# Cross attention: keys turned by DVE in blocks and placed by transfers through DRAM, for every batch but the first

## The reference

```python
q = x @ Wq.T
k_raw = context @ Wk.T          # context: 16 x 361 x 512
v_raw = context @ Wv.T
# heads of 16, 32 of them; k and v are the even and odd columns of [k_raw, v_raw]
q = _rmsnorm(q); k = _rmsnorm(k)      # t * rsqrt(mean(t*t over the 16) + 1e-6)
scores = einsum('bhnd,bhmd->bhnm', q, k) * 16 ** -0.5
out = einsum('bhnm,bhmd->bhnd', softmax(scores), v)
x = x + out
```

## Time and profile before

| | |
|---|---|
| median of 3 runs | 1312.95 us (1312.74 to 1315.94) |
| the profiled execution's own time | 1312.68 us |
| its span, first to last instruction | 1310.9 us |
| instructions | 27154 |
| busy: PE, DVE, ACT, POOL | 97%, 60%, 50%, 23% of the span |
| transfers | 63.98 MB in 18744 packets, mean 49 GB/s |

### The profile page before, as it was taken

One profiled execution on the slowest core, in us unless ns is written; L12 is line 12 of the kernel. 1 busy time (PEld: TensorE's weight loads), 2 busy tenths in 40 slices (PEclk: granted clock), 3 DMA queues, 4 the chain that ended last, 5 costly groups with the idle time before them and its releaser, 6 DMA issues.

```text
span 1310.9 us, 27154 instructions
## 1 busy us (share of the span) xinstructions
PE 1268.3 (97%) x10784; PEld 850.2 (65%) x10784; DVE 781.7 (60%) x1890; ACT 648.9 (50%) x1524; POOL 295.8 (23%) x293
## 2 busy tenths in 40 slices
PE   8989999999999999999999999999999999999998
PEld 7656666666666666566666666666666665666554
DVE  6897788777877787434344434554455784443423
ACT  4663344343433356377777776666665523232221
POOL 0564454334334451111101101111101121000000
PEclk9999999999999999999999999999999999999999
DMA  8102000000000021112222222001012310000000
GB/s 330 73 9 73 9 8 10 7 3 9 9 8 9 9 88 63 72 32 84 105 73 73 74 73 89 25 25 58 25 58 84 125 52 24 1 24 1 24 1 30
DMA packets 18744, 63.98 MB, mean 49 GB/s; under 512 B 1850, under 2 KB 3386, under 8 KB 15418
## 3 DMA queue, kind: packets, MB, share of 16 engines
q1 hardware_dynamic: 18618, 62.24, 13.4%
HBM read 55.68 MB, written 3.28 MB: 45 GB/s over the span
## 4 chain that ended last, share of the span: by engine, by line
PE 83%; DVE 6%; issue 5%; ACT 4%; POOL 2%; DMA 0%; POOLq 0%; SPq 0%; DVEq 0%; ACTq 0%
PE A L1861 18%; PE A L1761 11%; PE C L2214 10%; PE A L1824 10%; PE C L1892 6%; PE B L1912 4%; PE C L1789 3%; PE A L2233 3%; PE A L1842 3%; PE B L2233 2%; PE C L1806 2%; PE A L1770 2%; PE B L1781 2%; PE B L1878 1%; PE B L1797 1%
## 5 line engine op out<-in xcount | busy, mean ns | idle before, releaser
L1861 PE MATMUL A<-wxhl,arena 128*126 128x512 f16 x1104 | 254.7, 381 | 3.2 <-DVE arena L1221 2.6
L1861 PEld LDWEIGHTS A<-wxhl,arena 128*126 128x126 f16 x1104 | 145.4, 136 | 86.3 <-issue 8.1
L1761 PE MATMUL A<-arena,wxhl 128*125 128x512 f16 (+1 forms) x780 | 174.5, 380 | 1.3 <-DVE tub L1140 1.3
L855 ACT ACTIVATE arena<-C 126x1600 f32<-126x1600 f32 x96 | 144.4, 1504 | 22.3 <-PE C L1892 22.3
L595 POOL TENSOR_TENSOR arena<-arena,region 126x512 f32<-126x512 f32 (+2 forms) x59 | 60.9, 1062 | 405.8 <-DVE region L1282 405.8
L1761 PEld LDWEIGHTS A<-arena,wxhl 128*125 128x125 f16 (+1 forms) x780 | 103.5, 136 | 62.1 <-DVE tub L1140 5.3
L2214 PE MATMUL C<-arena 128*128 128x375 f16 (+1 forms) x768 | 138.8, 333 | 0.0
L758 ACT ACTIVATE region<-C,negm 100x100 f32<-100x100 f32 x256 | 84.3, 358 | 100.8 <-DVE negm L1183 100.8
L569 POOL TENSOR_TENSOR region<-tub 125x512 f32<-125x512 f32 (+1 forms) x65 | 82.5, 1269 | 219.3 <-DVE tub L1140 217.0
L1824 PE MATMUL A<-arena,stageb 128*125 128x512 f16 (+1 forms) x416 | 124.0, 379 | 2.1 <-ACT qk L829 1.3
L2214 PEld LDWEIGHTS C<-arena 128*128 128x128 bf16 x768 | 74.8, 97 | 58.8
(11 more groups left out here) (201 smaller groups left out, 2256.5 us busy)
## 6 DMA issues: line engine op xcount, KB each, us to landing
stageb<-in_wffn SPq DMA_DIRECT2D x16, 768.0 KB, 4.8
arena<-in_ctxt SPq DMA_DIRECT2D x16, 756.0 KB, 5.8
stageb<-in_wffn SPq DMA_DIRECT2D x8, 1024.0 KB, 6.2
arena<-in_wqkv SPq DMA_DIRECT2D x4, 1024.0 KB, 12.1
wxhl<-in_wffn SPq DMA_DIRECT2D x4, 1024.0 KB, 4.7
arena<-in_wx SPq DMA_DIRECT2D x3, 1024.0 KB, 8.4
out_x<-xres SPq DMA_DIRECT2D x12, 224.0 KB
xres<-in_wo SPq DMA_DIRECT2D x2, 1024.0 KB, 19.3
```

What stands on the lines that cost most here:

```text
L855: act.activation(e[:, at:at + 2].rearrange("p f (r s) -> p r f s", r=RT), Call[0:KC, :].rearrange("p (r x) -> p r x", r=RT)[:, :, 0:4 * S] ...
L1761: ins = pe.matmul(A[j % 2][0:m, :], xp[:, k, at:at + m], wp[:, j, k, :], start=(n == 0), stop=(n == 11))
L1861: ins = pe.matmul(A[(par + n) % 2][0:KC, :], xp[:, k, c * KC:(c + 1) * KC], wp[:, 1 if n < 4 else 2, k, :], start=(i == 0), stop=(i == 11))
```

## The change

For every batch but the first, keys are no longer turned by PE. DVE transposes the normed key tile raw[par][:, c] (128 x 512) in blocks of 32 x 32 into a staging tile kts[:, c] (turn_keys). SP then writes the staging tile to a DRAM buffer with four transfers, one for each block of 32 partitions (keys_out), whose addresses put each block of 32 x 32 at its place in the turned matrix: runs of 32 words of 4 bytes. The buffer for c = 0 and 1 is kd01, for c = 2 kd2, each twice, by the parity of the batch. When the writes have landed, one transfer reads kd01 into kTd, the new tile of turned keys, and another the batch's own columns of kd2 (keys_in); a third reads the shared tile's tail into the next batch's half of kTd (keys_shared). PE's scores wait for these transfers (kr01 ahead of unit 0; kr2 and krx ahead of unit 1). Batch 0 still goes through PE and ACT.

The norms are worked out in two parts of 64 columns (key tiles 0 and 1; key tile 2 and queries), each with its own signal to POOL, which now takes key tiles 0 and 1, then queries, then key tile 2. On DVE the ternary passes stand behind the second part, and turn_keys of tile 2 behind add_cross of the first half. PE's wait for last turn's add_cross moves from ahead of turn_heads(b,2) to ahead of x2_turn.

The diff, cut to its core:

```diff
-        kT = carve([128, 2, NT, CTXP])
+        kTd = carve([128, 2, NT, NC * KP])
...
+        kd01 = nc.dram_tensor("keys01", (2, 128, NT, 2, KP), F32).ap()
+        kd2 = nc.dram_tensor("keys2", (2, 128, NT, KP), F32).ap()
...
+            def keys_out(b, c):
+
+                sp.wait_ge(*count("d_kt", b, c + 1))
+                for n in range(4):
+                    block = slice(32 * n, 32 * n + 32)
+                    if c < 2:
+                        dst = kd01[b % 2].rearrange("(r j) t c n -> c j t r n", r=4)[c][:, :, :, block]
+                    else:
+                        dst = kd2[b % 2].rearrange("(r j) t n -> j t r n", r=4)[:, :, :, block]
+                    sp.dma_start(dst, kts[block, c].rearrange("j (t r i) -> j t r i", t=NT, r=4)).then_inc(kw[c], 16)
+
+            def keys_in(b):
+
+                for c in range(2 if short(b) else NC):
+                    keys_out(b, c)
+                sp.wait_ge(*written(0, b))
+                sp.wait_ge(*written(1, b))
+                sp.wait_ge(*count("pe_sc", b - 2, NU))
+                sp.dma_start(kTd[:, b % 2, :, 0:2 * KP], kd01[b % 2].rearrange("p t c n -> p t (c n)")).then_inc(kr01, 16)
+                if not short(b):
+                    sp.wait_ge(*written(2, b))
+                    own = own_rows(b)
+                    sp.dma_start(kTd[:, b % 2, :, 2 * KP:2 * KP + own], kd2[b % 2][:, :, 0:own]).then_inc(kr2, 16)
+
+            def keys_shared(b):
+
+                sp.wait_ge(*count("pe_sc", b - 1, NU))
+                own = own_rows(b)
+                src = kd01[b % 2][:, :, 1] if short(b) else kd2[b % 2]
+                sp.dma_start(kTd[:, 1 - b % 2, :, 2 * KP + own:2 * KP + KC], src[:, :, own:KC]).then_inc(krx, 16)
...
             for b in range(NB - 2):
                 if b < NB // 2:
                     sixteenth(2 * b, 0)
+                if b > 0:
+                    keys_shared(b)
+                if b < NB // 2:
                     sixteenth(2 * b + 1, 1)
                 context(b + 2)
+                keys_in(b + 1)
                 if b == NB // 2:
...
+            keys_shared(NB - 2)
...
                 tile(n)
+                if n == 3:
+                    keys_in(NB - 1)
...
-                pool.wait_ge(*count("d_rstd2", b, 1))
                 q = [(rows_of(q_tile(b)), 3, "g_qn")] if q_tile(b) is not None else []
                 last = 1 if short(b) else 2
-                for rows, slot, done in q + [(KC, c, "g_kn") for c in range(last + 1)]:
+                keys = [(KC, c, "g_kn") for c in range(last + 1)]
+                for rows, slot, done in keys[:2] + q + keys[2:]:
+                    pool.wait_ge(*count("d_rstd2", b, 1 if slot < 2 else 2))
...
-                    act.wait_ge(*count("pe_T", b - 2, 4))
+                    if b == 2:
+                        act.wait_ge(pe_T0, NT)
+                    act.wait_ge(*count("d_kt", b - 2, 3))
...
-            def keys_back(b, t):
-
-                act.wait_ge(*count("pe_T", b, t + 1))
-                own = own_rows(b)
-                tail = (1 if short(b) else 2) * KC
-                whole = 2 * KC if short(b) else tail + own
-                ins = act.activation(kT[:, b % 2, t, 0:whole], B[0][:, 0:whole], ACT.Copy)
-                if b < NB - 1:
-                    act.wait_ge(*count("pe_sc", b - 1, T_UNITS[t]))
-                    ins = act.activation(kT[:, 1 - b % 2, t, 2 * KC + own:CTXP], B[0][:, tail + own:tail + KC], ACT.Copy)
-                ins.then_inc(sig["a_T"], 1)
+            def first_keys_back(t):
+
+                act.wait_ge(pe_T0, t + 1)
+                own = own_rows(0)
+                act.activation(kTd[:, 0, t].rearrange("p (c n) -> p c n", c=NC)[:, :, 0:KC],
+                               B[0][:, 0:CTXP].rearrange("p (c n) -> p c n", c=NC), ACT.Copy)
+                act.activation(kTd[:, 1, t, 2 * KP + own:2 * KP + KC], B[0][:, 2 * KC + own:CTXP], ACT.Copy)\
+                   .then_inc(a_T0, 1)
...
-            def rms_start(b, par):
-
-                if q_tile(b) is not None:
+            def rms_start(b, part, par):
+
+                if part == 1 and q_tile(b) is not None:
                     dve.wait_ge(*count("d_ssqq", q_tile(b), 1))
-                dve.wait_ge(*count("d_ssq2", b, 3))
+                dve.wait_ge(*count("d_ssq2", b, 2 + part))
                 dve.wait_ge(*count("g_kn", b - 2, 3))
-                st.chain(dve.tensor_scalar(xssq, xssq, 1.0 / XD,
-                                           EPS_RMS * (SX * SW) ** 2, ALU.mult, ALU.add))
-                y = xrstd[par].bitcast(I32)
-                st.chain(dve.tensor_scalar(y, xssq.bitcast(I32), 1, None, ALU.logical_shift_right))
+                v = xssq[:, 64 * part:64 * part + 64]
+                st.chain(dve.tensor_scalar(v, v, 1.0 / XD, EPS_RMS * (SX * SW) ** 2, ALU.mult, ALU.add))
+                y = xrstd[par][:, 64 * part:64 * part + 64].bitcast(I32)
...
+            def turn_keys(b, c, par):
+
+                dve.wait_ge(*count("g_kn", b, c + 1))
+                dve.wait_ge(*written(c, b - 1))
+                dve.transpose(kts[:, c], raw[par][:, c])\
+                   .then_inc(sig["d_kt"], 2 if c == 1 and short(b) else 1)
...
+                if end < 2:
+                    rms_start(b + 1, 0, odd)
+                    for n in range(3):
+                        rms_step(0, odd, n == 2)
+                    if not short(b + 1):
+                        square_sums(b + 1, 3)
+                    turn_keys(b + 1, 0, odd)
+                    turn_keys(b + 1, 1, odd)
+                    rms_start(b + 1, 1, odd)
+                    for n in range(3):
+                        rms_step(1, odd, n == 2)
                 if b == NB // 2 + 1:
                     scales3()
                 if NB // 2 < b < NB - 1:
                     ternary(*divmod(b - NB // 2 - 1, 2))
-
-                if end < 2:
-                    if not short(b + 1):
-                        square_sums(b + 1, 3)
-                    rms_start(b + 1, odd)
-                    for n in range(3):
-                        rms_step(odd, n == 2)
-                else:
+                if end == 2:
...
                     add_cross(o2_tile(b), 0)
+                if end < 2 and not short(b + 1):
+                    turn_keys(b + 1, 2, odd)
...
-                    pe.wait_ge(*count("a_T", b, 1))
                     pe.wait_ge(*count("d_qT", last_tile(b), 1))
+                if b == 0 and u != 2 and u < 5:
+                    pe.wait_ge(a_T0, {0: 1, 1: 2, 3: 3, 4: 4}[u])
+                elif b > 0 and u == 0:
+                    pe.wait_ge(kr01, 16 * b)
+                elif b > 0 and u == 1:
+                    pe.wait_ge(*own_landed(b))
+                    if b == 1:
+                        pe.wait_ge(a_T0, 4)
+                    else:
+                        pe.wait_ge(krx, 16 * (b - 1))
...
-                if last_o2(b - 1) >= 0:
-                    pe.wait_ge(*count("d_on", last_o2(b - 1), 2))
-                elif b == 0:
+                if b == 0:
                     pe.wait_ge(*count("d_x2", 1, 1))
-                turn_heads(b, 2, par)
+                    turn_heads(0, 2, 0)
...
-                pe.wait_ge(*count("a_T", b, 3))
-                turn_heads(b, 3, par)
+                if b == 0:
+                    pe.wait_ge(a_T0, 3)
+                    turn_heads(0, 3, 0)
...
-                    if q_tile(b + 1) is not None:
-                        pe.wait_ge(*count("d_qT", q_tile(b + 1), 1))
-                    turn_heads(b + 1, 0, odd)
...
-                if end < 2:
-                    turn_heads(b + 1, 1, odd)
...
-                if end < 2:
-                    pe.wait_ge(*count("a_T", b + 1, 2))
+                if end < 2 and q_tile(b + 1) is not None:
+                    pe.wait_ge(*count("d_qT", q_tile(b + 1), 1))
```

More of the change, by code:

```diff
@@ L260, in build @@
         carve = carver()
-        raw = [carve([KC, 4, 512]) for _ in range(2)]
+        raw = [carve([128, 4, 512]) for _ in range(2)]
         ctxs = carve([128, KT, CTXP])
@@ L435, in build, with written, own_landed @@
         g_ones = sem("g_ones")
+        pe_T0, a_T0 = sem("pe_T0"), sem("a_T0")
+        kw = [sem(f"kw{c}") for c in range(NC)]
+        kr01, kr2, krx = sem("kr01"), sem("kr2"), sem("krx")
+        def written(c, b):
+            return kw[c], 4 * 16 * sum(c < 2 or not short(n) for n in range(1, b + 1))
+        def own_landed(b):
+            return kr2, 16 * sum(not short(n) for n in range(1, b + 1))
         d_warm, a_ws, g_wlo, a_z = sem("d_warm"), sem("a_ws"), sem("g_wlo"), sem("a_z")
@@ L1580, in _ @@
                 square_sums(0, n)
-            rms_start(0, 0)
-            for n in range(3):
-                rms_step(0, n == 2)
+            for part in range(2):
+                rms_start(0, part, 0)
+                for n in range(3):
+                    rms_step(part, 0, n == 2)
             normed2(1, rs1[:, 0:1])
@@ L1891, in scores2 @@
```

(16 more changed lines are left out.)

42 lines of the change are left out of this document (23 added, 19 removed).

## The result

The changed kernel takes **1386.24 us**, the median of 5 runs (1382.83 to 1387.51), against 1312.95 before; the ratio of the means, here as for every run below, is 1.0544, with a 95% interval of 1.0526 to 1.0563. It is 73 us slower; the prediction said 1409, with 1338 to 1540 as its range. Its profiled execution took 1387.05 us, with a span of 1385.3.

What follows compares the result with a forecast made beforehand. PE (TensorE), busy 97% of the span, was taken as the bound. 1312.7 - 24.3 (work off PE) + 80 (waits for keys) + 7 (ternary) + 33 (clock) = 1409 us, range 1338 to 1540.

Steps and rivals of the forecast that it cites:

- What goes from PE: Cross attention on PE: 172 transposes of keys and the 0.21 us waits for ScalarE's copy go, 24.3 us less.
- Wait for keys: PE's first scores of a batch wait for the keys' read: 5.0 us in 13 turns, 7.7 in two, 80 us.
- cheap packets: Rival for the keys' writes: at 7 to 15 ns a packet SP's order alone sets the wait; 1352 us, chance 0.25.
- x2_lo: Ternary passes on DVE now stand ahead of x2_lo, so PE's out_turn comes later in turns 9 to 14: 7 us.
- just covered: Turn 1: x2_lo ends at 604.6, when PE's out_turn wants it; each tenth of a slower step is paid.
- Clock: PE runs at a lower clock after each wait for keys: 2.2 us times 15, 33 us.
- 20 to 40 ns, 0.48: The forecast's own case for the price of a 128-byte packet, summed at 30 ns to 1409 us; chance 0.48.
- The signs: Expected in the profile: 15 waits for keys of 5 us, none for the second read, some 88,000 packets under 512 bytes.
- Hidden transfers: Rival: group 2's turn to the read's landing takes at most 3.2 us, PE never waits; 1296 us, chance 0.04.
- break-even: Case where group 2's turn to the read's landing takes about 4.8 us and the change gains nothing; chance 0.04.
- costs nothing but order: Extra DVE work of 2.4 us of norms and 2 us of turns a turn, in an engine busy 14 of 32 us.
- Dear packets: Rival for the keys' writes: about 50 ns a packet, waits of 12.6 us a turn, 189 us; 1510 us, chance 0.19.

Runs made afterwards that it cites:

- e3: The changed kernel without the three reads of turned keys and PE's waits for them, so scores work on zeros: 1318.64 us, ratio 1.0047.
- e2: The changed kernel with the read of groups 0 and 1 issued ahead of the four writes of group 2: 1333.63 us, ratio 1.0169.
- e5: The changed kernel with group 2 written by eight transfers of 16 partitions instead of four of 32, same 128-byte runs: 1417.9 us, ratio 1.0782.
- e4: The changed kernel with the ternary passes moved from between the norms and x2_lo to behind queries_back: 1380.66 us, ratio 1.0513.
- e1: The changed kernel with 14 products of unused result on PE ahead of its wait for the keys, batches 1 to 14: 1372.75 us, ratio 1.0454.
- e6: The changed kernel with the read ahead of group 2's writes, ternary passes behind queries_back, x2_lo ahead of the norms' second part: 1327.66 us, ratio 1.0109.
- e8: e6 with the read of groups 0 and 1 cut in two, 128 KB for unit 0 first, then the rest: 1315.5 us, ratio 1.0012.
- e9: e8 with ten products of unused result ahead of the first scores of the two short batches: 1311.78 us, ratio 0.9985.

## Why the prediction came out as it did

The direction, the first late step and the order of its causes were right. Of the four terms of the sum one was far off, one was half of what it should have been, and they erred in opposite directions. That the total came within 23 us is in part luck.

**What goes from PE: 24.3 predicted, 25.1 measured.** 172 transposes at 0.116 us (e3; 0.125 was taken) are 19.9 us, the 13 waits for ACT's copy 2.8. Not counted in the prediction were two waits of turn_heads for the turned queries, the 1.4 and 1.0 in the earlier trace rows, which also went: 2.4. The busy times agree: 21.0 us less at full rate.

**Wait for keys: 80 predicted, 47.9 measured.** The chain was the one described: second sum, norms (12 steps from 599.44 to 602.44, 3.0 us, 3.1 predicted), POOL (2.08 for two products), turns (0.71 each against 0.65), add_cross, the turn of group 2, four issues, the read, the scores. Two sizes in it were off. The mis-sized term is **the packet**: 30 ns was taken, 11.7 measured, so nothing queued behind the packets and the range's far end, 108 ns, was never near. What looked like a fixed cost of 23 ns in the difference between 2 KB writes and reads the earlier trace rows wasn't one. The other is the issue: 0.65 us against 0.59 taken. The wait of turn 1 is thus that of the rival "cheap packets", 3.0 worked out there and 3.36 measured; SP's order makes it, as e2 and e5 show from either side. Nor were the turns ahead of short batches the dear ones: 7.7 was predicted, measured were 4.0 in turn 6 and none in turn 13. There PE waits 4.9 us for x2_lo earlier in the turn, which covers it; the prediction priced each wait as though the other weren't there.

The page "DMA: Bandwidth & Descriptors" of the Trainium skill, section "Why small descriptors are slow (HBM only)", from which the prediction drew an estimate of 8 ns, is nearer to the 11.7 than the 30 taken from rows. The trace has 4 ns more than that estimate. It can't show whether the table's reading and rewriting under 512 bytes is part of it, since the whole price is small.

**x2_lo: 7 predicted, 16.2 measured (14.1 + 2.1).** That out_turn was "just covered" was read off turn 1, and there it holds: x2_lo is through at 608.79, out_turn comes at 609.23. Two things were left out. In turn 9 not only the ternary passes stand in its way but also eight small instructions of scales3, 2.4 us, which moved with them:

```profile
892.36 0.16 DVE L1368 TENSOR_SCALAR fsc<-fsc 128x3 f32<-128x3 f32 x1
...
895.62 1.28 DVE L1387 SCALAR_TENSOR_TENSOR early<-stageb,fsc,early 128x1024 bf16<-128x1024 f32 x1
896.82 0.67 DVE L1299 TENSOR_TENSOR tub<-B,tub 128x500 f16<-128x500 f32 x1
```

```profile
897.55 0.70 PE L2000 MATMUL B<-cst,alo 128*125 128x128 f32 x4 [3.94 <-DVE tub L1299]
```

And turns ahead of short batches, in which PE is some 4 us sooner while DVE's list is hardly shorter, were priced for the keys but not for x2_lo: turn 13 pays 4.9 us, turn 6 1.7. e4 splits the sum in halves.

**Clock: 33 predicted, 37.3 measured.** Taken was 2.2 us for each of fifteen waits, from bounds of 0 and 3.5. By the stretches 4.2 us lie behind the two longest waits for x2_lo, and the other 33.1 are 2.4 on average for the 14 waits for keys, between nothing (one wait of 2.66 us) and 5.8 (the last). e1 shows it to be a cost of its own and not another name for the wait. What the prediction had no row for, how long the clock stays down, is here: 3.4 us in turn 1, twice that in more than half of the turns. Its upper bound of 3.5 us of loss for a wait was passed once.

**The sum.** 1310.9 - 25.1 + 47.9 + 16.2 + 37.3 = 1387.2, against a span of 1385.3. The 1.9 too much is mostly a wait for ctx_lo of 2.6 us in the kernel before, which the new waits cover. The forecast was 23 us too high: 32 too much for the keys, 9 and 4 too little for x2_lo and the clock. It came that near because these errors offset each other. By mechanism the likeliest case wasn't the one named (20 to 40 ns, 0.48) but "cheap packets", worked out as 1352. That rival took the waits right (48) and missed on the clock (6 for 37) and x2_lo (10 for 16): it took a wait of 3 us to be nearly free of the second cost, and each of the 14 waits of 3.1 us or more in the changed kernel (12 for keys, 2 for x2_lo) has it behind it.

**The signs.** The new waits are there, 14 and not 15, 3.4 us on average and not 5, and none for the second read. PE's busy time rose, as foretold for a clock that dips. DVE's 43 turns take 0.71 us. Packets under 512 bytes are 107162, not near 88,000: that number counted the writes alone (43 x 2048), while the second and third reads also go in runs under 512 bytes; without the reads, in e3, they are 92666.

**Rivals on the other side.** "Hidden transfers" was worked out as 1296, and e3 is that case: 1318.6. So the place of break-even was wrong too; its 4.8 us is 3.2 + 24.3 / 15, which leaves out even the 8 us for ternary of the same paragraph. The step that fails is that DVE's extra work "costs nothing but order": x2_lo, ctx_lo and the clock behind them cost 27 us by e3's account (16.3 + 2.2 + 8.7), more than the 25.1 that PE was relieved of. Dear packets are excluded by the rate itself.

What a repaired version is worth was shown by e2, e6, e8 and e9: the whole loss of 73 us can be taken back, 59 of it by order alone (e6), but what is left is 0.15% below the kernel before. Whether DVE's list can be made short enough to keep more of the 25 us wasn't tried.

## What to carry to other kernels

When work is moved off the engine that bounds a kernel, follow the new road to the one queue in which it is issued: here a read that could have gone out at 611 went out at 614, because writes whose data came later stood ahead of it, and putting it first was worth 53 of 73 us. Price a wait on TensorE with what the clock takes afterwards (here, on average, 3.4 us of waiting and 2.4 more from slow work), and price all waits of a turn together, since one covers another: what e4 and e6 mended came back by half or more at the next wait. And count what the engine that takes over pays: 62 us of new work on DVE, "under" a PE that was busy 97%, was worth as much as all that PE was spared.

## What the runs showed of the hardware

- Writes to DRAM in runs of 128 bytes cost 11.7 ns a packet on each DMA engine (75 GB/s at a share of 0.43), and a transfer of 64 KB in 512 of them landed 2.2 us after its issue. I had expected 30 ns.
- SP's issue of such a transfer takes 0.64 to 0.67 us, whether it has 512 runs or 256 (2.59 us for four, 5.13 for eight). Between these two sizes the cost goes by transfer and not by run.
- Behind each of the 14 waits of TensorE of 3.1 to 4.9 us in the changed kernel the granted clock was at 0.50 (1.2 instead of 2.4 GHz), for 3.4, 6.8 to 6.9, or once 13.6 us. The 3.4 us stretches begin between 0.2 us before the end of the wait and 1.4 after it, the longer ones 0.5 to 2.1 us before it. Waits of up to 6.8 us (e5) cost no more, 2.3 us of loss on average.
- The length of a wait doesn't decide it. In the changed kernel the clock fell behind a wait of 2.11 us and not behind those of 2.12, 2.14 and 2.66; in e5 it fell behind one of 1.65, in e6 not behind one of 2.98, and in e4 not behind one of 3.38:

```profile
727.09 0.96 PE L1972 MATMUL C<-region,arena 32*126 32x200 f32 x16 [3.38 <-issue]
```

- After the same wait of 1.93 us it fell in one execution (e8, 0.79) and not in the other (e9, 1.00). What tips it is open. Products without use in the wait's place keep it up.
- DVE turns 128 x 512 f32 in blocks in 0.71 us, hardly more than the 0.68 of a sum over the same width.
